# A fused RWKV-7 and feed-forward kernel on one core: new order tables for how its work streams are interleaved

## The reference, cut to what matters

```python
xn = _layernorm(x)
# RWKV-7: seven mixed inputs and low-rank branches give r, w, k, v, a, b per token, then the scan
def step(S, inp):
    rt, dt, kt, vt, at, bt = inp
    sa = jnp.einsum('bhij,bhj->bhi', S, at)
    S = S * dt[:, :, None, :] + sa[..., None] * bt[:, :, None, :] + vt[..., None] * kt[:, :, None, :]
    y = jnp.einsum('bhij,bhj->bhi', S, rt)
    return (S, y)
# y is group-normalized, gets a bonus term, is gated and projected by w_output
s = ((y_norm + (rr * kr * time_faaaa).sum(-1) * vr) * g) @ w_output.T
# feed-forward with 8-bit weights that are scaled to float
h = jax.nn.silu(xn @ wg.T) * (xn @ wu.T)
g = jax.nn.silu(h @ wd.T)
x + s * g
```

## Time and profile before

| | |
|---|---|
| median of 3 runs | 1592.45 us (1587.87 to 1592.75) |
| the profiled execution, its own time | 1592.75 us |
| span of its instructions | 1591.3 us |
| mean granted TensorE clock | 0.984 of full speed |
| PE busy | 1495.3 us, 94% |
| DVE busy | 1266.4 us, 80% |
| ACT busy | 1096.4 us, 69% |
| POOL busy | 365.5 us, 23% |

### The profile page before, as it was taken

How to read it: one execution, slowest core, us unless ns; L and a number is a source line. 1 busy time by engine, 2 the same in 40 slices (tenths; PEclk the granted TensorE clock), 3 DMA queues, 4 the chain that set the end, 5 groups by cost and what they waited for, 6 DMA issues and landing times.

```text
span 1591.3 us, 56452 instructions
## 1 busy us (share of the span) xinstructions
PE 1495.3 (94%) x24384; PEld 1025.2 (64%) x24384; DVE 1266.4 (80%) x2661; ACT 1096.4 (69%) x1904; POOL 365.5 (23%) x362
## 2 busy tenths in 40 slices
PE   3579999999999999999999999999999999989887
PEld 1246767576676757666676676767676666756765
DVE  2778888888888878888888888888888888888633
ACT  3759587686858768586776858677685867758422
POOL 3020311313031131402213140221314022130101
PEclk9799999999999999999999999999999999999998
DMA  4011120301112030110302111130211103011120
GB/s 150 14 20 21 35 48 17 62 19 33 35 29 53 17 62 20 34 35 22 60 16 46 35 35 34 24 58 17 46 35 34 35 22 60 17 33 34 18 52 28
DMA packets 251462, 58.37 MB, mean 37 GB/s; under 512 B 223696, under 2 KB 250704, under 8 KB 251088
## 3 DMA queue, kind: packets, MB, share of 16 engines
q1 hardware_dynamic: 241936, 41.95, 14.0%
q10 hardware_dynamic: 9280, 12.81, 2.2%
HBM read 36.38 MB, written 18.35 MB: 34 GB/s over the span
## 4 chain that ended last, share of the span: by engine, by line
PE 76%; DVE 9%; POOL 5%; issue 4%; ACT 3%; DVEq 0%; ACTq 0%; POOLq 0%
PE bank L536 19%; PE chunk L380 12%; PE bank L546 11%; PE bank L511 4%; PE chunk L644 3%; PE chunk L616 3%; PE chunk L600 3%; PE chunk L591 3%; POOL big L1286 3%; PE bank L666 3%; PE chunk L630 2%; PE bank L485 2%; POOL st L1333 2%; DVE hat L1240 2%; PE bank L479 2%
## 5 line engine op out<-in xcount | busy, mean ns | idle before, releaser
L1327 POOL TENSOR_TENSOR SF<-ST,CT 128x256 f32<-128x256 f32 x128 | 112.9, 882 | 630.6 <-DVE ST L1213 630.6
L536 PE MATMUL bank<-xT,wg 128*128 128x256 f32 x768 | 202.8, 396 | 13.5 <-DVE VU L983 13.5
L536 PE MATMUL bank<-xT,wu 128*128 128x256 f32 x768 | 202.4, 395 | 0.6 <-issue 0.6
L546 PE MATMUL bank<-wd,hT 128*128 128x256 f32 x768 | 177.4, 384 | 0.9 <-DVE hT L1173 0.8
L536 PEld LDWEIGHTS bank<-xT,wg 128*128 128x128 f32 x768 | 136.2, 190 | 57.5 <-DVE VU L983 24.1
L546 PEld LDWEIGHTS bank<-wd,hT 128*128 128x128 f32 x768 | 144.6, 192 | 28.2 <-DVE hT L1173 8.2
L536 PEld LDWEIGHTS bank<-xT,wu 128*128 128x128 f32 x768 | 138.7, 191 | 29.5 <-issue 8.2
L380 PE MATMUL chunk<-KS,W 128*128 128x512 f32 x320 | 149.1, 597 | 0.0
L889 ACT ACTIVATE Y<-chunk 32x256 f32<-32x256 f32 x256 | 96.1, 375 | 54.6 <-PE chunk L600 51.9
L380 PE MATMUL chunk<-big,W 128*112 128x512 f32 (+1 forms) x256 | 117.1, 599 | 6.7 <-ACT gT L721 3.4
L863 ACT ACTIVATE sg<-bank 128x512 f32<-128x512 f32 x96 | 57.2, 596 | 79.6 <-PE bank L536 78.6
(11 more groups left out here) (156 smaller groups left out, 3325.4 us busy)
## 6 DMA issues: line engine op xcount, KB each, us to landing
smalls<-in_x SPq DMA_DIRECT2D x32, 256.0 KB, 3.1
Y<-in_x SPq DMA_DIRECT2D x32, 256.0 KB, 2.9
out<-fsil ACTq DMA_DIRECT2D x32, 256.0 KB, 2.3
scrA<-AM SPq DMA_DIRECT2D x64, 64.0 KB, 2.0
hat<-scrB SPq DMA_DIRECT2D x32, 128.0 KB, 3.0
hat<-scrF SPq DMA_DIRECT2D x32, 128.0 KB, 3.2
KE<-scrA SPq DMA_DIRECT2D x64, 32.0 KB, 2.1
scrT<-KE SPq DMA_DIRECT2D x16, 128.0 KB, 1.7
```

What stands on the lines that cost most here:

```text
L536: q = pe.matmul(o[:, TT_ * n2:TT_ * n2 + TT_], w[:, h, 128 * (n + n2):128 * (n + n2) + 128], x_now[:, h], start=(h == 0), stop=(h == NH - 1))
L546: q = pe.matmul(o[:, 256 * m:256 * m + 256], hT[:, n, 128 * m:128 * m + 128], wd[:, n, :], start=(n == 0), stop=(n == NF - 1))
L1327: pool.tensor_tensor(SF[:, :, :, :], ST[:, :, :, :], fade[:, c].unsqueeze(3).to_broadcast([128, B, NH, N]), ALU.mult).then_inc(*faded.up)
```

## The change

Only the tables are changed. Every stream has the same steps with the same instructions as before; the sum over all engines is the same but for the table loads of ACT, which are put in wherever the kind of function changes. A pass of ACT has ten of them before and nine after.

```diff
-ORDER = {"pe": ("NNNNFKOONFNOKKVNONNNRKVRBKBNNRNNBBNNVBBNBNBVBBNBBEBNBBVBBNBBVBBXBNBBNBBXBXBBNBXBBNNBXBBXNBBLBXBBXNBB"
-                "XLXXXLL"),
...
+ORDER = {"pe": ("NNNFNKOOFNNOKVONNNNKVKRRBKBNNRNNNBBNBBVBNNBVBBNBBEBNBBVBBNBBVBXBBNNBXBBNBBXBXBBNBBNBXBBXNBBLBXBBXNBB"
+                "LXXXXLL"),
...
```

More of the change, by code:

```diff
@@ L51 @@
 CTOT = _at
-ORDER = {"pe": ("NNNNFKOONFNOKKVNONNNRKVRBKBNNRNNBBNNVBBNBNBVBBNBBEBNBBVBBNBBVBBXBNBBNBBXBXBBNBXBBNNBXBBXNBBLBXBBNXBB"
-                "XLXXXLL"),
[L55 to L61, removed]
+ORDER = {"pe": ("NNNFNKOOFNNOKVONNNNKVKRRBKBNNRNNNBBNBBVBNNBVBBNBBEBNBBVBBNBBVBXBBNNBXBBNBBXBXBBNBBNBXBBXNBBLBXBBNXBB"
+                "LXXXXLL"),
+         "act": ("NFKFFFFFOFNNKVKOVKKKBERBKKXRRXDBXBNNVBVBBVVBNBBXBBBVXBBBVNBXBBXBBLBXLBLBBXNBBLXX"),
+         "dve": ("ONBOOBBBBBOBBDBBBBDBBDDBNBBOKKXFEDKDDDKNEEXKEEXBBXXNXBXXBXXXBXXXBEEXXBXXXXBNLBXBLXXBXBXXNXXXXXXBXBXB"
+                "LLXBBXLLLLLLLL"),
+         "pool": ("DBBBBBLBLBBBLLLLLLLL")}
+FIRST = {"pe": ("NNFKFVKKVNKNNRNNNRVKNNNNVNNNNVVREXNNXXXLXXNNXXNNXNLNNXXXLNLNN"),
+         "act": ("FKFFNFFFNKFNKNVVKKEKRVVVNKXDKRXVRXVXLVNXNLXLXXXXLNX"),
+         "dve": ("DNDDDDKKEDNDFDNKKNEENXXLKXEXXEXXEXXXXXXELXXXXXXXXXXXXXXXXNXXLLXXXXXLLLLLLLL"),
          "pool": ("DLLLLLLLLLL")}
-LAST = {"pe": ("NNNONONONONNNNNNBBNNNBBBBBNBBBBBNBNBBNBBNBBBNBBNBBBBBNBBBBBNBBBBBBBBNBBNNN"),
-         "act": ("NNBNBBBOOBBBNBBBBBNBBBBNBBBBBBNBBBBBN"),
-         "dve": ("BOOOBBBBNBBBBBBBBBBBBNOONBBBBBBBBNBBBBNBBBBNB"),
+LAST = {"pe": ("NNNNNONONNNOONNNBBNNNBBNBBBBBNBBBBBBNBBBBNBBBBBBNNBBBBBNBBBBNBBBBBBNBBNNNN"),
+         "act": ("NNNBBOBBBBOBBNBBBBBBBBNBNBBBBBBBBBNBN"),
+         "dve": ("BONOOBBBBBBBBBBBBBBBBONONBBBBBBBBNBBBNBBBBBNB"),
          "pool": ("BBBBBBBBB")}
```

## The result

The changed kernel takes 1601.28 us (median of 7 executions, 1597.99 to 1606.16), the one before 1587.87 beside it (7 executions, 1583.3 to 1594.99): a ratio of 1.0094, 95% interval 1.0066 to 1.012, or 13 us by these medians. The forecast was no change. One of 24 executions of the changed kernel on record, with 1624.5 us, is left out everywhere; the other 23 have a mean of 1603.8, against 1587.2 in 102 of the kernel before, which makes the loss 16.6 us.

What follows compares the result with a forecast made beforehand. PE was taken to bound the kernel; terms -5.1 - 2.7 + 4.5 + 1.5 - 0.5 + 0.5 = -1.8 us from 1592.75 led to a forecast of 1590.5 us, no change; own range 1586 to 1597, with rivals 1578 to 1605.

Steps and rivals of the forecast that it cites:

- What bounds the kernel: Whole kernel: PE, busy 1495.3 of 1591.3 us, no other engine above 80%; PE has no slack to hide a wait.
- A: PE's chunk walk: more y and u products side by side save net 0.34 us a pass, -5.1 (-6 to 0).
- B: PE's wait before band (L565) for transfer L1393: an earlier flip on DVE cuts it, -2.7 us (-3.7 to 0).
- C: DVE's next-tile statistics ahead of chunk 4's copy: late input delays PE's s, +4.5 us (0 to +18).
- D: ACT and DVE around the chunks: moved table load and silu, later copies of u, +1.5 us (0 to +6).
- the rival on it: ACT's moved table load costs 1.4 us more ahead of chunk 1's copies: +18, so 1608.5 us; chance 0.04.
- E: The ends: passes -1 and 0 -0.5 us (-3 to +3); pass 16 and last chunks +0.5 (-3 to +4).
- The rival on the last passes: PE waits for the up product, then runs both down products at low clock: +7, so 1597.5 us; chance 0.07.
- The start of the sum: The profiled execution of the kernel before, 1592.75 us, to which the forecast added its terms.

Runs made afterwards that it cites:

- stats_behind: Changed kernel with the next tile's statistics moved behind chunk 4's addition on DVE, chunk 5's copy, a key step, root and chunk 5's addition directly behind: 1.0158, 1612.5 us.
- stats_behind2: The same altered kernel (statistics behind chunk 4's addition, against the changed kernel), run again for a profile of an undisturbed execution: 1624.9 us with one long product.

## Why the prediction was wrong, step by step

- **What bounds the kernel**: right. PE's busy time did not change, its standing did.
- **A, neighbours on PE**: right in itself. In chunks 3 to 5 the middle pass is 0.39 us shorter (0.34 forecast), -5.8 in fifteen passes. (B and C below are the sums over twelve passes, times 15/12.)
- **B, band**: right. 3.0 us in twelve passes, 3.8 in fifteen, against 2.7. The store that follows the flip is done 0.4 us earlier in the pass (0.7 forecast for the flip), the load lands 0.7 earlier. Not seen: F's second step now stands 0.55 us in each pass before L420, since it needs the bank that ACT empties of k0 and two halves no longer stand between. What PE gains at out0 and k1 (0.31 and 0.10) and at a half (0.11) pays for it.
- **C, the statistics**: right in mechanism and size, 3.0 us in twelve passes, 3.8 in fifteen, against 4.5; DVE waits at L945 in eight passes.
- **D, ACT and DVE tight**: mis-sized. In chunks 0 to 2 the middle pass is 0.3 us longer, which is 4.6 and not 1.5. Two thirds of it are at values2, u2 and up12, where copies come later: ahead of "values" (L591) PE and its weight loads wait for ACT's copy of y (L889) 57 times in the kernel after, 25.3 us, and 39 times in the one before, 19.9. The other third is vT0 in a new place, 1.09 in place of 0.98, a cost of neighbours that A had not counted. No run takes D away by itself. It is no table load: each still takes 1.28 us, and the rival on it did not come. ACT's loads at L870, kernel after:

```profile
L870 ACT ACT_TABLE_LOAD  x15: 1283/1283/1283, 144.9 to 1466.8; - x15
```

- **Missing from ORDER's sum**, a step that failed: the stops for instructions, +5.6. The trace before had them; I had read them as chance ("issue") and priced the pairs of y and u without asking what stands around them. With this the sum is -5.8 - 3.8 + 3.8 + 4.6 + 5.6 = +4.4, at the lower edge of the measured +8.4 (4 to 13). What the other 4 us are stays open; the long products may be part of it.
- **E, the ends**: the step that failed most. "LAST +0.5 (-3 to +4)" is +10, outside its bounds. The rival on the last passes (+7, at 0.07) had the mechanism, PE waiting and then the low clock, but at the down products; it was the corrections and the chunk walk. The third up step does wait for the product behind the flip, as the text of E says: 4.64 us in the kernel after, and 2.24 more at band, directly ahead of the corrections. The kernel before stood as long in this pass, 3.3 and 1.9 us, but behind those waits came both output products and seven halves of gate and up, the last six of them directly ahead of band. I had counted waits and not what they do to the clock of the work behind them, though the earlier trace rows showed the same eight instructions at 3.75 in place of 1.9.
- **The start of the sum**, 1592.75, held one long product, and its chance was not in the text.

The two that failed, the missing stops and E, are about 6 and 10 us; everything I had listed for the twelve passes came within about 3.

## What to carry to other kernels

A wait of PE can cost twice, where the work behind it then runs at half clock (13.7 us for 9.3 here): when steps are moved, look in every stretch with slack at what PE does directly ahead of the dense part, and keep its own filler work there. Before placing small matrix products side by side, look for idle times of "issue" that come at equal counts of instructions: here such stretches were bounded by how fast instructions arrive. And one profile of each is too little where chance events of 3 to 6 us are as large as the change; lengths of single steps, by the median over passes, told the two apart.

## What was not expected of the hardware

- PE's instruction stream comes over a queue of its own (194 packets, 3.18 MB in the kernel after), and PE can stop when the count of all its records is 192 past a multiple of 256, for up to 1.6 us.
- DVE can lose three more instructions of POOL after the one under way: 4.97 in place of 1.43 us.
- One execution of stats_behind took 4848 us: each of passes 2 to 14 took 299.5 us, and PE's long steps up to 3.9 times as long as in stats_behind2, with the granted clock shown as 1.00. The profile gives no cause.
